# 64-column tiles for the plain float32 matmuls of a mixture-of-experts layer and a GRU

## The reference

```python
# layer 0: a shared gated MLP and 8 experts, of which each token takes 2
shared = silu(xf @ w1) * (xf @ w3) @ w2
s = sigmoid(concat([xf, tf]) @ router_W)            # tf: the conditioning vector of the batch row
gates = top-2 shares of s + router_bias
h = gelu(einsum('nc,ech->enh', xf, W1e)); y = einsum('enh,ehc->enc', h, W2e)
x = x + (shared + sum_e gates_e * y_e) / 3
# layer 1: a GRU over the 512 steps, state H of shape (8, 256)
Z = sigmoid(x @ Wxz.T + bxz + H @ Whz.T + bhz)
R = sigmoid(x @ Wxr.T + bxr + H @ Whr.T + bhr)
Ht = tanh(x @ Wxh.T + bxh + (R * H) @ Whh.T + bhh)
H = Z * H + (1 - Z) * Ht
out = x + H @ Whq.T + bhq
```

## Time and profile before

| | |
|---|---|
| median of 3 runs | 1370.22 us (1368.84 to 1370.8) |
| profiled execution | 1367.91 us |
| its span, first to last instruction | 1366.1 us |
| PE busy, matmul records | 1333.9 us (98%), 35606 |
| PE weight loads | 912.0 us (67%), 35606 |
| VectorE busy | 1015.9 us (74%) |
| ScalarE busy | 808.2 us (59%) |

### The profile page before, as it was taken

How to read it: one execution, slowest core, us unless ns; L and a number is a source line. 1 busy time by engine, 2 the same in 40 slices (tenths; PEclk the granted TensorE clock), 3 DMA queues, 4 the chain that set the end, 5 groups by cost and what they waited for, 6 DMA issues and landing times.

```text
span 1366.1 us, 83284 instructions
## 1 busy us (share of the span) xinstructions
PE 1333.9 (98%) x35606; PEld 912.0 (67%) x35606; DVE 1015.9 (74%) x5797; ACT 808.2 (59%) x4395; POOL 8.2 (1%) x26
## 2 busy tenths in 40 slices
PE   7989999999999999999999999999999999999997
PEld 7666666667666666666666666666666666766554
DVE  4558877777777777777777777777777777777655
ACT  4136556566666666666666666666666666665554
POOL 1000000000000000000000000000000000000000
PEclk9999999999999999999999999999999999999999
DMA  8410100101111010101001010100101111010110
GB/s 259 132 26 16 31 25 20 41 10 42 19 31 25 22 40 10 43 20 31 25 22 40 10 42 19 36 23 21 38 10 42 20 42 20 25 31 10 42 20 11
DMA packets 43400, 47.56 MB, mean 35 GB/s; under 512 B 7192, under 2 KB 38424, under 8 KB 43032
## 3 DMA queue, kind: packets, MB, share of 16 engines
q1 hardware_dynamic: 43032, 42.25, 12.3%
HBM read 25.46 MB, written 16.78 MB: 31 GB/s over the span
## 4 chain that ended last, share of the span: by engine, by line
PE 92%; DVE 4%; ACT 3%; issue 1%; DMA 1%; SPq 0%
PE up_ps L958 26%; PE zc_bank L1058 22%; PE dn_ps L931 20%; PE r_bank L1058 12%; PE aux L931 4%; PE misc L931 4%; PE up_ps L931 2%; DVE t_rT L811 1%; DVE rhT L814 1%; ACT t_r L558 1%; ACT x1T L517 1%; DMA xT_all<-in_L_cond_w 1%; ACT t_h L578 1%; DVE terms L832 0%; ACT gru_raw L459 0%
## 5 line engine op out<-in xcount | busy, mean ns | idle before, releaser
L578 ACT ACTIVATE t_h<-zc_bank 128x32 f32<-128x32 f32 x1024 | 146.2, 194 | 251.8 <-PE zc_bank L1058 251.7
L558 ACT ACTIVATE t_r<-r_bank 128x32 f32<-128x32 f32 x1024 | 146.7, 195 | 220.1 <-PE r_bank L1058 208.1
L931 PE MATMUL dn_ps<-we_sb,hid_e 128*32 128x256 f32 x4096 | 269.1, 379 | 1.4 <-DVE x_all L715 1.4
L1058 PEld LDWEIGHTS r_bank<-whT,hist 128*8 128x8 f32 x8192 | 118.5, 88 | 190.0 <-DVE hist L835 185.5
L832 DVE STREAM_TRANSPOSE terms<-t_h 128x32 f32<-128x32 f32 x1024 | 156.5, 192 | 114.5 <-ACT t_h L578 107.2
L811 DVE STREAM_TRANSPOSE t_rT<-t_r 128x32 f32<-128x32 f32 x1024 | 156.1, 191 | 109.0 <-ACT t_r L558 72.5
L1058 PE MATMUL zc_bank<-whT,rhT 128*8 128x64 f32 x8192 | 212.0, 219 | 11.0 <-DVE rhT L814 8.6
L1058 PE MATMUL r_bank<-whT,hist 128*8 128x64 f32 x8192 | 211.7, 220 | 2.6 <-DVE hist L835 0.9
L1058 PE MATMUL zc_bank<-whT,hist 128*8 128x64 f32 x8192 | 209.5, 219 | 1.1 <-issue 1.1
L1058 PEld LDWEIGHTS zc_bank<-whT,rhT 128*8 128x8 f32 x8192 | 132.5, 88 | 97.9 <-ACT t_z L560 28.1
L958 PE MATMUL up_ps<-x_high,we_low 128*128 128x256 f32 x512 | 157.2, 307 | 0.7 <-issue 0.7
(11 more groups left out here) (125 smaller groups left out, 1680.9 us busy)
## 6 DMA issues: line engine op xcount, KB each, us to landing
gate_inputs_by_token<-gru_raw SPq DMA_DIRECT2D x32, 384.0 KB, 2.3
gru_raw<-gate_inputs_by_token SPq DMA_DIRECT2D x256, 48.0 KB
x_all<-in_x SPq DMA_DIRECT2D x32, 128.0 KB
out<-gru_raw SPq DMA_DIRECT2D x32, 128.0 KB
x_all<-in_L_cond_W1e SPq DMA_DIRECT2D x1, 2048.0 KB, 12.1
we_sb<-in_L_cond_W2e SPq DMA_DIRECT2D x1, 2048.0 KB, 13.2
xT_all<-in_L_cond_w SPq DMA_DIRECT2D x2, 512.0 KB, 6.1
w_sb<-in_L_cond_w SPq DMA_DIRECT2D x1, 512.0 KB, 8.0
```

The costliest lines, as they stand in the source:

```text
L558: act.activation(t_r[:, i, :], r_ps[:, i * Q:(i + 1) * Q], ACT.Tanh, scale=0.5).then_inc(tr_ready, 1)
L578: act.activation(t_h[:, i, :], c_ps[:, i * Q:(i + 1) * Q], ACT.Tanh, scale=-1.0).then_inc(th_ready, 1)
L931: done = pe.matmul(ps[Q * j:Q * (j + 1), col:col + cols], lhsT[:, Q * j:Q * (j + 1)], rhs, start=first, stop=last, tile_position=(0, Q * j ...
L1058: done = pe.matmul(ps[Q * j:Q * j + B, :], lhsT[:, k, :], whT[:, gate, k, j * GW:(j + 1) * GW], start=False, stop=(k == NI - 1), tile_posi ...
```

## The change

`product` cuts its 128 output partitions into two tiles of 64 in place of four of 32. The gates keep tiles of 32, the up-projections of 128. The same columns are computed from the same operands.

```diff
     Q = 32
+    WIDE = 64
...
             def product(ps, col, cols, lhsT, rhs, first, last):
 
-                for j in reversed(range(NG)):
-                    done = pe.matmul(ps[Q * j:Q * (j + 1), col:col + cols], lhsT[:, Q * j:Q * (j + 1)], rhs,
-                                     start=first, stop=last, tile_position=(0, Q * j), skip_group_check=True)
+                for j in reversed(range(P // WIDE)):
+                    done = pe.matmul(ps[WIDE * j:WIDE * (j + 1), col:col + cols], lhsT[:, WIDE * j:WIDE * (j + 1)], rhs,
+                                     start=first, stop=last, tile_position=(0, WIDE * j), skip_group_check=True)
                 return done
```

## The result

| | before | after |
|---|---|---|
| median of 4 runs | 1370.51 us (1368.84 to 1371.83) | 1435.91 us (1433.66 to 1437.47) |
| ratio | | 1.0477, 95% interval 1.0456 to 1.0497 |
| profiled execution, span | 1367.91, 1366.1 us | 1437.47, 1435.7 us |

The change makes the kernel slower by 65 us; 1445 was forecast, within 1403 to 1476. First the page of after: the totals and the granted clock, which answer to the earlier trace rows, then the chain, answering to the earlier trace rows.

The account below looks back on a forecast made before the run. The chain over the other engines was taken to bound nearly every scan step, the products leaving 0.09 us slack. 1367.9 + 74 + 0.6 = 1442.5 us, 2.3 more on the median's scale: 1445 us, range 1403 to 1476.

Parts of the forecast that it names:

- The bound and the slack: Scan steps: the chain over other engines releases the reset gate; the products' streaming ends only 0.09 us ahead of it.
- (a): Products in the scan: eight fewer matmuls per pair of slots save zero, streaming stays 4 x 0.217 us.
- (b), (d): Width changes into and out of the products: each stops TensorE some 0.10 us; candidate to reset gate 1.36, not 1.19.
- The rival without a stop: Between widths 32 and 64 TensorE doesn't stop, the scan still releases the reset gate: 1370 us, chance 0.12.
- (c): First load after a width change is bared, 0.05 us for 64 columns; later loads hide under the 0.217 rounds.
- the rival of loads between the rounds: 64-column loads in the products don't hide, three more rounds wait 0.05 each: 73 us more, 1518 us, chance 0.03.
- (e): Scan: 468 steps with products, each 0.165 us later, 77 us; late steps give back 3, leaving +74.
- The late tanh of one round per turn: First tanh of each turn, 0.13 us late today, is hidden by the later reset gate: 15 x 0.13 = 2 us back.
- (f): Outside the main scan term: larger first loads in the opening's 14 groups and one change behind late logits, together +0.6 us.
- The signs: Trace: period 2.62 with products, 2.46 without; products start at 0.34; `hist` waits under 20 us; PE busy falls against span.
- same: Whole kernel: a time within about 0.2% of no change, chance 0.11.
- the four cases that end slower: Both stops 0.78, one stop 0.04, loads between rounds 0.03, the two tiles one after the other 0.01.

Follow-up runs that it names:

- cols192: The changed kernel with the scan's 256-column products streaming only 192 columns: 1363.59 us, ratio 0.9969 to the kernel before.
- cols192_w32: The changed kernel with the scan's products streaming 192 of 256 columns and tiles set back to 32: 1369.66 us, ratio 0.9993 to the kernel before.
- mix64_128: The kernel before, but in every second scan gap the first slot's product in tiles of 64, the second's as one tile of 128: 1527.73 us, ratio 1.1156.
- disjoint: The kernel before with only `keep_busy` changed: four 256-column matmuls on zeros, tiles alternately 32 and 64 wide, the first two sharing no column: 1537.4 us, measured once.
- opening64: The changed kernel with `product` in tiles of 64 only before the scan, 32 within it: 1370.21 us, ratio 1.0001 to the kernel before.
- The first three experiments: first64, mix64_128 and full128, which gave `product` other tile widths: 1444.85, 1527.73 and 1455.58 us.
- cols224: The changed kernel with the scan's 256-column products streaming only 224 columns: 1389.63 us, ratio 1.0154 to the kernel before.
- first64: The kernel before, but in every second scan gap the first slot's product in tiles of 64, the second's in 32: 1444.85 us, ratio 1.0553.
- full128: The changed kernel with every `product` as a single tile of 128 columns, everywhere: 1455.58 us, ratio 1.0633 to the kernel before.

## Why the prediction was right

*The bound and the slack.* Right. The granted clock of the scan stayed at 2.4 GHz, which the sum had as its condition (1.00 from 30 us on in the trace of after). cols192 shows it most directly: with the end of the products moved ahead of the scan, the stops are free.

*(a) Instructions.* The rounds are 0.22 with two tiles as with four. The forecast gave fewer instructions no value and left out the irregular waits. They are shorter after: adding up what the 511 intervals between reset gates in each trace have over the usual of their round gives 7.0 us before and 2.2 after. Whether the lower number of instructions does that or the stops, is open (cols192_w32).

*(b), (d) Two stops.* Right: 0.34 to the load, and 1.355 from gate to gate where 1.36 stood. The stop itself is nearer 0.09 than 0.10: the trace of after has 0.307 from the start of the last matmul to the next load in nearly every step, and the streams follow each other at 0.216. The Trainium skill's rule (page TensorEngine Tiling (Array Packing), section Tiling Modes, Key Properties) that changing the mode, not merely the tile, drains the engine holds here between 32 and 64 columns, with 0.34 against 0.22 us to the first product, and between 64 and 128 (mix64_128), and in tiles that don't touch (disjoint). The rival without a stop is out.

*(c) Loads.* Right: 0.05 bared with 64 columns. Later loads hide under the streams, the rounds stay 0.22; so the rival of loads between the rounds is out, and with it, for column tiles, the Trainium skill (page TensorE: Matmul & The Clock Gate, Part 3, The mechanism) in its claim that a load overlaps running matmuls only in another row group (the same section also excepts a load for the background weight buffer, and no run here shows whether these are such loads). The up-projections, which use all rows and follow each other at 0.12, spoke against it in the trace of before already.

*(e) The number of steps.* 467 steps in the trace have work of `product` behind the candidate gate, 468 were counted. Their usual interval went from 1.195 to 1.355, 0.160 in place of 0.165: 74.7 us. The late tanh of one round per turn is hidden now (the usual interval of that round, 2.60 before, is 2.62 like the others), 2.0 us back, as forecast. The irregular waits give 4.8 back, where 1 was put down. Sum 67.9; the scan, from first to last reset gate, grew from 1267.8 to 1335.4, by 67.6.

*(f) The opening part.* 1.95 us later in this one profile, with the lower clock. opening64 shows no cost of the tiles there, but its interval (0.9984 to 1.0019) is too wide to tell the forecast's 0.6 us from none. 67.6 and 1.95 make the 69.6 us between the spans.

The forecast was 5 us too high for the profiled execution (1442.5 against 1437.47): 2.5 from the step and its number, 3.8 from the irregular waits and 0.6 from (f), less the 1.95 of the opening. For the median it was 9 too high. The further 4 are chance: the forecast added 2.3 because the profiled execution of before lay that far under its median, and that of after lay 1.6 over its own. The first three experiments and cols224 were also 3 to 5 us under their forecasts, the way the irregular waits point; the kernel before was 1 to 2 us faster in those sets, which is a part of it.

*The signs.* The period (2.62 with products, 2.46 without) and the start of the products came as written. Two signs were wrong. PE's busy time was to fall against the span and rose, from 1333.9 of 1366.1 us to 1413.6 of 1435.7 (97.6% and 98.5%): the drawn end of a matmul, 0.38 after its start, reaches over the next load at 0.31, so a stop leaves no gap in the busy time. And the waits of the reset gate's load for `hist` were to fall under 20 us, and they did not (185.5 before):

```profile
PEld r_bank L1059 <- DVE hist L836: 181.9, 482, 1.0
```

The view names the last semaphore that the instruction waited for, and a stop has none of its own; where nothing else is waited for, it stands as "issue" (disjoint). Whether it set the start shows in the times alone: the scan ends at 702.49, the load is at 702.61.

*The chances.* The case without a stop stood at 0.12, "same" at 0.11, and the four cases that end slower add up to 0.86 where 0.87 stood; the text gives no reason for the 0.01.

## What to carry to other kernels

Count the changes of tile width on TensorE's queue, not only its instructions: in these kernels each cost about 0.09 us of standstill and one bared load, and a split into narrow tiles that looks wasteful can be there to keep one width across neighbours. What such a stop costs in time is what exceeds the slack of the chain beside it, so work that out first; streams shorter by 25% made two stops per step free. A busy share of 98% tells nothing of that, and a wait's named releaser has to be checked against the time at which the releaser was done.

## What the runs showed of the hardware

A change of column-tile width stops all of TensorE. Behind a last matmul of 256 columns the next load comes 0.31 us after its start, of which 0.22 are streaming: so it is from 64 to 32 (after, first64), from 64 to 128 (mix64_128), from 128 to 32 (full128) and from 32 to 64 (disjoint), there also for tiles without a common column. The stop doesn't grow with the stream. Medians over the scan, from the start of the last matmul to the next load, are 0.147 us behind 64 columns (32 to 64 and 32 to 128), 0.201 behind 128, 0.281 behind 224 and 0.307 behind 256 (64 to 32), and 0.09 us stay when the streams (0.055, 0.108, 0.189 and 0.216) are taken off; the two between are worked out from 0.216 by the number of columns. The bared load is 0.02, 0.05 and 0.11 us for 32, 64 and 128 columns. And in kernels with tiles of 64 or 128 in the scan's products PE's unexplained waits are 0.2 to 2.1 us, with tiles of 32 they are 12.3 to 19.9, about 1% of the time. They can stand beside other waits: between before and after the intervals of the scan show 4.8 us of difference, 0.3%.
